# Attention scores in four single banks: one exponential per head instead of one per pair of heads

## The reference, cut to what matters

```
scores = einsum('bhqd,bhkd->bhqk', Q, K) * softplus(temp)     # Q, K have unit length per head
attn = softmax(scores, axis=-1)
out = einsum('bhqk,bhkd->bhqd', attn, V) ...
return _lin(out, Wo, bo)
```

## Time and profile before

| | us |
|---|---|
| median of 3 runs (lowest, highest) | 1556.19 (1556.0, 1557.84) |
| the profiled execution, its own time | 1554.14 |
| its span in the trace | 1552.1 |
| mean granted TensorE clock, share of full | 0.889 |

### The profile page before, as it was taken

How to read it: one execution, slowest core, us unless ns; L and a number is a source line. 1 busy time by engine, 2 the same in 40 slices (tenths; PEclk the granted TensorE clock), 3 DMA queues, 4 the chain that set the end, 5 groups by cost and what they waited for, 6 DMA issues and landing times. The chain is left out here.

```text
span 1552.1 us, 19098 instructions
## 1 busy us (share of the span) xinstructions
PE 1169.3 (75%) x5854; PEld 411.3 (26%) x5854; DVE 1044.0 (67%) x1175; ACT 866.4 (56%) x943; POOL 407.6 (26%) x233
## 2 busy tenths in 40 slices
PE   5657777776588786667353999899899899678877
PEld 3222222222233332223053111111111111133333
DVE  5979999999589885999665133233224222589886
ACT  4864444443243332111043999899999999534333
POOL 3135555555234431666400000000000000043331
PEclk7868898989799997887775999999999999889998
DMA  2000000000100010000001011011011001000001
GB/s 65 0 1 0 0 0 0 0 0 0 41 28 1 27 28 22 1 0 0 6 2 29 8 34 25 17 36 27 18 23 38 20 20 25 22 28 27 27 28 54
DMA packets 23302, 28.29 MB, mean 18 GB/s; under 512 B 7266, under 2 KB 11874, under 8 KB 23266
## 3 DMA queue, kind: packets, MB, share of 16 engines
q1 hardware_dynamic: 23266, 27.85, 7.1%
HBM read 13.15 MB, written 2.10 MB: 10 GB/s over the span
## 5 line engine op out<-in xcount | busy, mean ns | idle before, releaser
L1595 ACT ACTIVATE att_prob<-att_s_ps 128x1024 f32<-128x1024 f32 x512 | 470.8, 1449 | 11.1 <-PE att_s_ps L1557 10.9
L1567 PE MATMUL att_o_ps<-att_prob,att_va 128*32 128x512 f32 x2048 | 278.2, 617 | 2.0 <-ACT att_prob L1595 2.0
L1557 PE MATMUL att_s_ps<-att_q_st,att_k_st 32*128 32x512 f16 x1024 | 193.9, 393 | 51.6 <-ACT att_prob L1595 12.2
L284 PE MATMUL scan_y_ps<-scan_hc,all_ident 128*128 128x512 f32 x256 | 153.5, 732 | 79.6 <-POOL scan_hc L626 63.6
L605 DVE TENSOR_TENSOR_SCAN scan_state<-scan_decay,scan_drive 128x1024 f32<-128x1024 f32 x64 | 207.8, 3248 | 0.2 <-ACT scan_decay L576 0.2
L626 POOL TENSOR_TENSOR scan_hc<-scan_state,scan_c_rep 128x1024 f32<-128x1024 f32 x64 | 154.5, 2415 | 149.4 <-DVE scan_state L605 144.7
L1620 DVE RECIPROCAL hv_h_seq<-hv_h_seq 32x1024 f32<-32x1024 f32 (+1 forms) x20 | 105.3, 5266 | 84.6 <-DMA hv_h_seq<-hv_h_seq 84.6
L1634 DVE COPY hv_h_seq<-att_o_ps 128x512 f32<-128x512 f32 x32 | 22.1, 689 | 201.9 <-PE att_o_ps L1567 201.9
L874 ACT ACTIVATE ffn_hid<-ffn_h_ps,ffn_be 128x1024 f32<-128x1024 f32 x64 | 71.3, 1113 | 146.5 <-PE ffn_h_ps L294 78.3
L580 ACT ACTIVATE scan_c_rep<-scan_c_ps 128x1024 f32<-128x1024 f32 x64 | 65.4, 1022 | 151.7 <-PE scan_c_ps L284 151.5
L992 DVE TENSOR_TENSOR ffn_hid_lo<-ffn_hid,ffn_hid_hi 128x1024 f16<-128x1024 f32 x96 | 147.3, 1535 | 3.3
(11 more groups left out here) (215 smaller groups left out, 1451.6 us busy)
## 6 DMA issues: line engine op xcount, KB each, us to landing
ffn_w1e<-in_w1e SPq DMA_DIRECT2D x16, 256.0 KB, 3.0
ffn_w2e<-in_w2e SPq DMA_DIRECT2D x16, 256.0 KB, 3.2
att_q_st<-hv_part SPq DMA_DIRECT2D x64, 64.0 KB, 2.1
att_k_st<-hv_part SPq DMA_DIRECT2D x64, 64.0 KB, 2.1
hv_h_seq<-hv_h_seq SPq DMA_DIRECT2D x96, 32.0 KB
ln_x_half<-in_x SPq DMA_DIRECT2D x8, 256.0 KB, 3.0
out<-store_out SPq DMA_DIRECT2D x8, 256.0 KB, 2.5
hv_h_seq<-hv_h_seq SPq DMA_DIRECT2D x64, 16.0 KB
```

Of the source, the lines that this page charges most:

```text
L284: last = pe.matmul(out[:, h], w, rhs[:, h], start=start, stop=stop)
L1557: last = pe.matmul(s_ps[n % 3][:, i, :], k_st[rows, g % 2, kc * P:(kc + 1) * P], q_st[rows, g % 2, HALVES[half]], start=True, stop=True)
L1567: last = pe.matmul(o_ps[half][32 * j:32 * j + 32, :], va[:, g % 2, kc, j, :], prob[:, u % RING, j, :], start=kc == 0, stop=kc == KC - 1)
L1595: act.activation(prob[:, u % RING, 2 * pair:2 * pair + 2, :], s_ps[n % 3][:, :, :], ACT.Exp).then_inc(exped.sem, 1)
```

## The change

The scores of one head get a buffer of their own. `s_ps` becomes one tile of four banks instead of three buffers of two banks, so it takes four banks of PSUM where it took six. `scores(g, u, j)` makes one head's scores with one matmul, numbered `n = (g * U + u) * 4 + j`, into bank `n % 4`, and each such matmul waits by itself for the exponential four before it and signals `scored` by itself. ScalarE takes one exponential of 128 x 512 for each head, 1024 of them instead of 512 of 128 x 1024. The projection goes into banks 0 and 1 in front of unit 15, after the exponential that last read bank 1. The matmuls, their number and shapes, the order of scores and values, the ring of `prob`, the DMAs and VectorE's work stay as they were.

```diff
-        s_ps = [q.ps(f"s_ps{k}", [P, 2, HALF]) for k in range(3)]
+        BANKS = 4
+        s_ps = q.ps("s_ps", [P, BANKS, HALF])
...
-        scored = q.count("scored", G * U * 2)
-        exped = q.count("exped", G * U * 2, 3)
+        scored = q.count("scored", G * U * GH)
+        exped = q.count("exped", G * U * GH, BANKS)
...
-                    def scores(g, u, pair):
+                    def scores(g, u, j):
                         half, kc = divmod(u, KC)
-                        n = (g * U + u) * 2 + pair
-
-                        pe.wait_ge(exped.sem, exped.before(b, n, 3 if n >= 2 else 2))
-                        if n == 2 * OUT_AT:
-                            project(b, n % 3)
+                        n = (g * U + u) * GH + j
+
+                        if n == GH * OUT_AT:
+                            pe.wait_ge(exped.sem, exped.before(b, n + 1, BANKS))
+                            project(b)
                             pe.wait_ge(added.sem, added.before(b, 0, 1))
-                        for i in range(2):
-                            rows = slice(32 * (2 * pair + i), 32 * (2 * pair + i) + 32)
-                            last = pe.matmul(s_ps[n % 3][:, i, :], k_st[rows, g % 2, kc * P:(kc + 1) * P],
-                                             q_st[rows, g % 2, HALVES[half]], start=True, stop=True)
-                        last.then_inc(scored.sem, 1)
+                        pe.wait_ge(exped.sem, exped.before(b, n, BANKS))
+                        rows = slice(32 * j, 32 * j + 32)
+                        pe.matmul(s_ps[:, n % BANKS, :], k_st[rows, g % 2, kc * P:(kc + 1) * P],
+                                  q_st[rows, g % 2, HALVES[half]], start=True, stop=True).then_inc(scored.sem, 1)
...
-                            for pair in range(2):
-                                scores(g, u, pair)
+                            for j in range(GH):
+                                scores(g, u, j)
...
-                            for pair in range(2):
-                                n = (g * U + u) * 2 + pair
+                            for j in range(GH):
+                                n = (g * U + u) * GH + j
                                 act.wait_ge(scored.sem, scored.at(b, n))
-                                if pair == 0:
+                                if j == 0:
                                     act.wait_ge(used.sem, used.before(b, g * U + u, RING))
-                                act.activation(prob[:, u % RING, 2 * pair:2 * pair + 2, :], s_ps[n % 3][:, :, :],
+                                act.activation(prob[:, u % RING, j, :], s_ps[:, n % BANKS, :],
                                                ACT.Exp).then_inc(exped.sem, 1)
```

More of the change, by code:

```diff
@@ L1534, in _, with project @@
                 pe.wait_ge(w_loaded, 16)
-                pe.matmul(s_ps[0][:, 0, 0:1], wo[:, :], t.col("bv"), start=True, stop=True).then_inc(bias_steps, 1)
+                pe.matmul(s_ps[:, 0, 0:1], wo[:, :], t.col("bv"), start=True, stop=True).then_inc(bias_steps, 1)
                 pe.wait_ge(bias_steps, 2)
-                def project(b, k):
+                def project(b):
                     for h in range(2):
                         pe.wait_ge(normed.sem, normed.before(b, G - 1 + h, G + 1))
-                        last = pe.matmul(s_ps[k][:, h, :], wo[:, :], att[:, HALVES[h]], start=True, stop=True)
+                        last = pe.matmul(s_ps[:, h, :], wo[:, :], att[:, HALVES[h]], start=True, stop=True)
                     last.then_inc(projected.sem, 1)
                 with pe.Fori(0, B) as b:
-                    def scores(g, u, pair):
+                    def scores(g, u, j):
                         half, kc = divmod(u, KC)
-                        n = (g * U + u) * 2 + pair
-                        pe.wait_ge(exped.sem, exped.before(b, n, 3 if n >= 2 else 2))
-                        if n == 2 * OUT_AT:
-                            project(b, n % 3)
+                        n = (g * U + u) * GH + j
+                        if n == GH * OUT_AT:
+                            pe.wait_ge(exped.sem, exped.before(b, n + 1, BANKS))
+                            project(b)
                             pe.wait_ge(added.sem, added.before(b, 0, 1))
-                        for i in range(2):
-                            rows = slice(32 * (2 * pair + i), 32 * (2 * pair + i) + 32)
-                            last = pe.matmul(s_ps[n % 3][:, i, :], k_st[rows, g % 2, kc * P:(kc + 1) * P],
-                                             q_st[rows, g % 2, HALVES[half]], start=True, stop=True)
-                        last.then_inc(scored.sem, 1)
+                        pe.wait_ge(exped.sem, exped.before(b, n, BANKS))
+                        rows = slice(32 * j, 32 * j + 32)
+                        pe.matmul(s_ps[:, n % BANKS, :], k_st[rows, g % 2, kc * P:(kc + 1) * P],
+                                  q_st[rows, g % 2, HALVES[half]], start=True, stop=True).then_inc(scored.sem, 1)
                     def values(g, u):
@@ L1564, in values @@
                             pe.wait_ge(out_done.sem, out_done.before(b, g * 2 + half, 2))
-                        pe.wait_ge(exped.sem, exped.at(b, (g * U + u) * 2 + 1))
+                        pe.wait_ge(exped.sem, exped.at(b, (g * U + u) * GH + GH - 1))
                         for j in range(GH):
@@ L1580, in _ @@
                         values(G - 1, u)
-                pe.wait_ge(exped.sem, exped.at(B - 1, G * U * 2 - 1))
-                project(B, 0)
+                pe.wait_ge(exped.sem, exped.at(B - 1, G * U * GH - 1))
+                project(B)
             @block.scalar
@@ L1604, in _ @@
                 dve.wait_ge(bias_steps, 1)
-                dve.tensor_tensor(bias[:, :], s_ps[0][:, 0, 0:1], t.col("bo"), ALU.add).then_inc(bias_steps, 1)
+                dve.tensor_tensor(bias[:, :], s_ps[:, 0, 0:1], t.col("bo"), ALU.add).then_inc(bias_steps, 1)
                 dve.wait_ge(blank, 1)
@@ L1644, in body @@
                         dve.wait_ge(projected.sem, projected.at(b + 1))
-                        k = 0 if isinstance(b, int) and b == B - 1 else 2 * OUT_AT % 3
-                        dve.scalar_tensor_tensor(t.x_t[:, b, :], s_ps[k][:, :, :].rearrange("p h c -> p (h c)"),
+                        dve.scalar_tensor_tensor(t.x_t[:, b, :], s_ps[:, 0:2, :].rearrange("p h c -> p (h c)"),
                                                  bias[:, 0:1], t.x_t[:, b, :], ALU.add, ALU.add).then_inc(added.sem, 1)
```

## The result

| | before | after |
|---|---|---|
| median, us | 1556.1 (4 runs, 1555.61 to 1557.84) | 1606.07 (4 runs, 1600.72 to 1607.36) |
| ratio, 95% interval | | 1.0313 (1.0288 to 1.0337) |
| profiled execution, us (span) | 1554.14 (1552.1) | 1600.72 (1598.7) |
| first to last exponential, us | 490.4 | 542.1 |

The changed kernel is slower by 50.0 us, where 40.6 was forecast: inside the range, with one term of the sum badly wrong. That it still lies inside is luck: the upper end, 1610, was priced for longer hand-overs, which did not come. The profiled execution after is the fastest of its four, 5 us under their median. In the profiles of this case the first exponential begins anywhere from 844.9 to 854.0 us, though nothing ahead of it is changed in any kernel.

The account below looks back on a forecast made before the run. The prediction took ScalarE to bind the kernel. Its terms, 31.3 + 3.3 + 3.2 + 2.4 + 0.4 = 40.6 us, on the median of 1556.2 gave 1596.8 us, range 1588 to 1610.

Parts of the forecast that it names:

- the upper end, 1610: Top of the main case: one hand-over longer by 0.1 us in TensorE's loop, 13 us more.
- exponentials: On ScalarE, two 512-column exponentials at 0.489 us each replace one of 0.916, all on the path: +31.3 us.
- TensorE's loop: With four banks, waiting for the previous unit's last exponential makes a unit 1.970 us instead of 1.956: +3.3 us.
- projection: At the projection, queued exponentials cover 0.59 us instead of 1.38, four times: +3.2 us.
- low clock at batch starts: At 1.2 GHz one two-unit loop per batch takes 5.25 us, 1.3 over ScalarE's pace, against about 0.7 now: +2.4 us.
- end and start of a batch: The third of the last units' values starts about 0.1 us late per batch, +0.4 us; table loads and first matmuls unchanged.
- Rival A: On ScalarE, the fixed part is that of SBUF-reading activations, 0.52 us an activation: 1626 us; chance 0.05.
- Rival D: On ScalarE, a short activation's fixed part hides entirely between neighbours, 0.425 us each: 1549 us; chance 0.02.
- One sign that I had named: ScalarE idle a little in nearly every unit, released by the scores; over 0.05 us each or never would refute the loop.
- Rival B: Hand-overs between TensorE and ScalarE are longer, 13 us for each 0.1 in the loop; two give 1623; chance 0.05 beyond 1610.
- the shorter first exponential might keep the clock up: At batch starts, a shorter first wait might keep TensorE's clock up: -3 us instead of +2.4.
- Rival C: TensorE's clock falls to 1.2 GHz throughout, 2.62 us a unit: 1759 us; in one batch of four, 1640; chance 0.03.

Follow-up runs that it names:

- run 1: Kernel before with each 1024-column exponential split into two of 512; banks, waits and signals as before: 1585.67 us, ratio 1.0201.
- Run 8: Kernel before with two buffers of three banks, mostly 1536-column exponentials for three heads, and the projection on its own turn: 1543.85 us, ratio 0.9925.
- Run 7: Kernel before with the projection taking its own turn among the three double banks, the wait for the sum two pairs later: 1551.53 us, ratio 0.9967.
- run 2: Changed kernel with heads 0 and 1 of a unit sharing one TensorE wait, 64 wait instructions less in a batch's loop body: 1599.45 us, ratio 1.0279.
- run 5: Kernel before with an increment of an unread semaphore before each pair of scores, 128 more TensorE instructions in a batch's body: 1567.4 us, ratio 1.0076.
- run 4: Changed kernel with six single banks instead of four: 1597.7 us, ratio 1.0258.

## Why the prediction was right, and where it was wrong

In the table, "measured" is the change in the stretch between the exponentials. The first line is run 1 against the kernel before. The others are the changed kernel against run 1, read from the starts and ends of ScalarE's records; the two paces are means over 40 undisturbed units.

| term | forecast | measured |
|---|---|---|
| exponentials | +31.3 | +31.4 |
| TensorE's loop | +3.3 | (1.9667 - 1.9600) x 256 = +1.7 |
| projection | +3.2 | +4.0 |
| low clock at batch starts | +2.4 | +3.9 |
| low clock after a projection | not seen | +1.9 |
| end and start of a batch | +0.4 | +8.8 |
| sum | +40.6 | +51.7 |

*Exponentials.* Right, and from the nearest rows: copies out of PSUM, not activations that read SBUF. Rival A fell with run 1; the fixed part of the Trainium skill (ScalarE: Activation LUTs, "What ACT_TABLE_LOAD costs") would have made it +48, and the run shows 31.4. Run 8 shows the same term with its other sign. Rival D, that it hides entirely, fell too.

*TensorE's loop.* The mechanism is right and shown twice: with six banks the unit is 1.960, ScalarE's pace, with four 1.966, and with two double banks 3.82 for two units as added up. The term was half of what I said, for two small reasons of about equal size: ScalarE's own pace is 1.960 and not 1.956, and two units of the loop come to 3.93 and not 3.94 (the release in the earlier trace rows is 0.05, where I took 0.06). One sign that I had named did not come: outside its stalls ScalarE shows next to no idle time, 0.1 us in the whole attention. By that sign the loop would have been refuted. It was a bad sign, for neighbouring exponentials overlap by 0.1 us in the records, and a delay of 0.01 leaves no gap; the difference between runs with six and with four banks shows it. Rival B, longer hand-overs from four signals in place of two, fell: the unit is 1.966, below the 1.970 that was worked out with no longer hand-over.

*Projection.* Right: the cover is what counts. Against the kernel before, from which the forecast was worked out, the four stalls are 3.3 us longer; run 1 had already made them 0.8 shorter, which is why the table has 4.0. Why they are shorter there was not looked into. Run 7 shows the cover from the other side.

*Low clock at batch starts.* Mechanism right, size off. I had one disturbed loop in each batch, 1.3 us; the changed kernel shows that one and, in batches 1 to 3, a second of 0.4. The spell at the low clock also lasts longer there, 10.2 us instead of 6.8, but this is the smaller part: with the short body (run 2) the spell is back to 6.8, and the disturbed loops cost only some 0.5 us less in all. That the shorter first exponential might keep the clock up did not come true.

*Start of a batch: the step that failed.* I wrote "Table loads, the first matmuls, DVE's copies, DMAs: unchanged, and hidden as before". The first matmuls of batches 1 to 3 are not unchanged. The change gives TensorE 128 more waits in a batch's body, and the working priced the added signals in time (at nothing) and nowhere that added waits are instructions which must be loaded. For the end and start of the batches 0.4 us was forecast and 8.8 measured. Run 2 takes this stall away and run 5 brings it in with nothing else touched, and both the 2.8 to 3.4 us and the packets on q8 follow. Part of it was to be had before: the profile page of the kernel before shows 18 packets for the whole program, so the body stayed loaded; how much longer it could grow, no line of it told. The Trainium skill (Runtime: NRT & Kernel Launch, "Instruction fetch mechanics") says that instructions come in blocks of 16 KiB, 256 instructions, by a DMA of the sequencer's own, and that a taken branch to a target outside what is loaded stalls. The trace agrees on the blocks, 0.75 MB in 46 packets being 16 KB each, and on the stall at the branch. It does not bear out the two blocks to which the Trainium skill there limits what is loaded: the kernel before branches back over 1700 instructions without a packet. By the size that the Trainium skill gives there for TensorE, 2048 instructions, the changed body of 1828 would have passed; here it did not. Nine packets a batch are, as an estimate from the Trainium skill's 256 instructions a block, one block more than those 2048. So where the body lies on the blocks may count as well as its length; no run here moves it. As a rival with its own place and a price it belonged in the prediction, though only the runs give the price.

*Rival C*, the low clock throughout, did not come. A small part of it did: after the projection of batch 1, TensorE was at 1.2 GHz for 6.8 us, +1.9 us. In the kernel before and with six banks, no batch shows that. TensorE's idle time after the projection does not decide it. It is 1.57 us in the changed kernel, where the clock falls in one batch, and 1.57 with six banks, where it never falls; it is 1.49 in run 2, where it falls in two batches, and 1.49 in the kernel before, where it never falls.

Left open: why the low clock after the projection comes in one batch of the changed kernel, in two of run 2 and in none of run 4.

## What to carry to other kernels

Count an activation's fixed part against the number of activations: where ScalarE binds, fewer and wider ones are the direction, as far as banks allow (1024 of 512 columns: +31 us in the stretch; 344 of mostly 1536: -12 in the stretch, some 3 of them from the better-placed projection). Add up the loop from one engine's release back to itself, over as many rounds as the buffers are deep, before shrinking buffers; it came out right within a hundredth of a microsecond. And when an edit adds waits or splits instructions in a hardware loop, look at the packets of the instruction queues: on TensorE a body just past what stays loaded cost some 3 us at every branch back.

## What the runs showed of the hardware that I had not expected

Between 65 and 127 more instructions in TensorE's loop body lies an edge. Counting one batch in the traces, weight loads, matmuls and sequencer's instructions together, 1700 (before) and 1765 (run 2) stay loaded, with 18 and 19 packets in the whole program; 1827 (run 4) and 1828 (after, run 5) do not, with 46, and the restart of the loop takes 2.8 to 3.6 us more. Whether the edge is one of length alone, or also of where the body begins, is not shown. On ScalarE a body loaded again in each batch cost nothing that the profile shows (451 instructions in run 1, 579 in run 2). That it had its next instructions before the first scores came would explain this, but no run here separates it.
